# LayerNorm rows on ScalarE, shared low halves in eight blocks, a first x tile of its own, two counts ahead of a finish

## The reference, cut to what matters

```python
def reference(x, adj, W, b, gate_w, w1, w2, w3, sw1, sw2):   # x 2048x256, adj 2048x2048
    deg = maximum((adj != 0).sum(-1), 1)
    x = x + gnn(layernorm(x), adj, deg, W, b)
    x = x + ffn(layernorm(x), gate_w, w1, w2, w3, sw1, sw2)

def gnn(x, adj, deg, W, b):
    a_norm = rsqrt(deg) * (adj + eye) * rsqrt(deg)
    return relu((a_norm @ x + x) @ W + b)

def ffn(x, ...):                   # 8 experts of 256 -> 1024 -> 256, top 1, and a shared one
    comb = one_hot(argmax(x @ gate_w.T)) * softmax(its logit)
    y = sum over experts of (silu(x @ w1.T) * (x @ w3.T) * comb) @ w2.T
    return y + gelu(x @ sw1.T) @ sw2.T
```

## Time and profile before

| | us |
|---|---|
| median of 3 runs | 507.82 (506.71 to 508.75) |
| the profiled execution's own time | 510.69 |
| its span (first to last instruction) | 509.1 |
| PE busy, DVE, ACT, POOL | 457.6, 270.9, 197.2, 322.3 |
| mean granted clock of TensorE | 0.966 of full |

### The profile page before, as it was taken

How to read it: one execution, slowest core, us unless ns; L and a number is a source line. 1 busy time by engine, 2 the same in 40 slices (tenths; PEclk the granted TensorE clock), 3 DMA queues, 4 the chain that set the end, 5 groups by cost and what they waited for, 6 DMA issues and landing times.

```text
span 509.1 us, 8980 instructions
## 1 busy us (share of the span) xinstructions
PE 457.6 (90%) x2652; PEld 391.9 (77%) x2653; DVE 270.9 (53%) x558; ACT 197.2 (39%) x434; POOL 322.3 (63%) x299
## 2 busy tenths in 40 slices
PE   5899977999999989899687999699979999999992
PEld 5778756897789878798565888588868888888871
DVE  4997799917692569767451343233423333343330
ACT  3555721663456454745241333122322232232230
POOL 3889865487857786576065584857475848887111
PEclk9999989999999999999897999799989999999997
DMA  7574150503160251719869777787878787465000
GB/s 255 185 217 154 49 165 13 165 2 117 49 206 1 76 174 43 253 42 321 233 198 322 240 249 257 257 267 232 276 237 280 241 274 232 56 71 73 8 1 0
DMA packets 40876, 82.61 MB, mean 162 GB/s; under 512 B 4880, under 2 KB 16528, under 8 KB 38800
## 3 DMA queue, kind: packets, MB, share of 16 engines
q1 hardware_dynamic: 25792, 45.11, 28.8%
q0 software_dynamic: 7536, 29.39, 18.9%
q10 hardware_dynamic: 7520, 7.77, 4.9%
HBM read 74.74 MB, written 8.41 MB: 163 GB/s over the span
## 4 chain that ended last, share of the span: by engine, by line
PE 41%; DVE 15%; DMA 11%; POOL 10%; issue 6%; ACT 2%; SPq 1%; POOLq 0%; DVEq 0%; ACTq 0%
PE bank L1208 16%; DMA eraw<-in_experts 7%; POOL ering L413 6%; PE bank L1233 6%; PE bank L1126 5%; DVE count L729 4%; PE bank L1145 4%; DMA ering<-in_experts 4%; POOL a_lo L366 3%; DVE rows L705 3%; PE bank L1234 3%; PE bank L1219 2%; PE bank L1147 2%; PE bank L1040 1%; DVE resid L795 1%
## 5 line engine op out<-in xcount | busy, mean ns | idle before, releaser
L413 POOL TENSOR_TENSOR ering<-eraw,ering 128x512 fp32r<-128x512 f32 x84 | 105.7, 1286 | 75.1 <-DMA ering<-in_experts 37.4
L1208 PE MATMUL bank<-ering,xsT_hi 128*128 x368 | 125.8, 414 | 11.6 <-POOL ering L413 7.5
L366 POOL TENSOR_TENSOR a_lo<-araw,a_hi 128x512 fp32r<-128x512 f32 x64 | 93.6, 1480 | 30.3 <-ACT a_hi L500 30.1
L1040 PE MATMUL bank<-zz,a_hi 128*128 128x512 f32 (+1 forms) x256 | 93.3, 404 | 7.0 <-POOL a_lo L366 6.9
L1208 PEld LDWEIGHTS bank<-ering,xsT_hi 128*128 128x128 f32 x368 | 72.1, 196 | 29.4 <-issue 12.7
L959 DVE SCALAR_TENSOR_TENSOR hid<-bank,xs,sil 128x512 f32<-128x512 f32 x46 | 34.5, 751 | 111.0 <-ACT sil L625 109.0
L1208 PE MATMUL bank<-ering,xsT_lo 128*128 x184 | 75.0, 408 | 0.0
L625 ACT ACTIVATE sil<-bank 128x512 f32<-128x512 f32 x46 | 27.5, 599 | 119.7 <-PE bank L1208 119.7
L1042 PE MATMUL bank<-zz,a_lo 128*128 128x256 f32 (+1 forms) x256 | 72.2, 282 | 0.0
L1233 PE MATMUL bank<-ering,hidT_hi 128*128 x184 | 67.8, 408 | 1.2 <-DVE hidT_lo L967 1.2
L1040 PEld LDWEIGHTS bank<-zz,a_hi 128*128 128x128 f32 x256 | 48.8, 191 | 20.0 <-issue 8.4
(11 more groups left out here) (151 smaller groups left out, 809.4 us busy)
## 6 DMA issues: line engine op xcount, KB each, us to landing
eraw<-in_experts SPq DMA_DIRECT2D x96, 256.0 KB, 3.3
araw<-in_adj_t SPq DMA_DIRECT2D x32, 512.0 KB, 5.0
ering<-in_experts POOLq DMA_DIRECT2D x8, 1536.0 KB, 7.4
ering<-in_experts POOLq DMA_DIRECT2D x8, 1024.0 KB, 7.1
ering<-in_experts POOLq DMA_DIRECT2D x8, 512.0 KB, 5.9
xs<-sorted_x ACTq DMA_DIRECT2D x23, 129.0 KB
resid<-in_x SPq DMA_DIRECT2D x4, 512.0 KB, 8.8
sw_raw<-in_sw_t ACTq DMA_DIRECT2D x2, 1024.0 KB, 7.0
```

Of the source, the lines that this page charges most:

```text
L366: pool.tensor_tensor(a_lo[:, u % AR, :], araw[:, u // CJ, u % CJ, :], a_hi[:, u % AR, :].bitcast(F32), ALU.subtract).then_inc(adj_lo_ok, 1)
L413: pool.tensor_tensor(ering[:, slot, 1, c * ECW:(c + 1) * ECW], eraw[:, c % ER, :], ering[:, slot, 0, c * ECW:(c + 1) * ECW].bitcast(F32), ...
L1040: pe.matmul(acc(it)[:, :], a_hi[:, s, it * P:(it + 1) * P], zt, start=first, stop=False)
L1208: ins = pe.matmul(bank[2 * w + h][:, :], a[:, k, :], ering[:, bass.ds(slot, 1), part, at:at + BANK].rearrange("p a n -> p (a n)"), start=n ...
```

## The change

It has four parts.

- **Rows on ScalarE.** Except for the first four tiles, a norm's row is no longer a DVE instruction (L705) but an ACT one, `Identity(rstd * x + shift)` with two operands per partition. DVE makes `shift = -mean * rstd` for four tiles in one instruction (`scales`) after the reciprocal. In the front, ACT makes the row of tile t+2 after `z_high(t)`; for quarters 1 to 3 `stds` moves ahead of `a_hi` of tile 11, and the four rows come after that `a_hi`. For the last quarter the four rows come right after `stds`.
- **Low halves in eight blocks.** `sw1_lo` and the low half of `sw2_r` were one instruction each of 2048 elements. They become eight and eight of 256, each with its semaphore count; blocks 0 to 3 now after the second four counts of quarter 1, blocks 4 to 7 after `choose(0)`. PE waits for the blocks one by one; before, for all of them ahead of `gate(0)`.
- **First x tile alone.** SP loads x tile 0 (128 KB), chunk 0, x tiles 1 to 3 (384 KB), chunk 1, x group 1, chunk 2, group 2, chunk 3, group 3; before, group 0, group 1, chunk 0, group 2, chunk 1, group 3, chunk 2, chunk 3. ACT and DVE norm tile 0 alone, split W, split the transposed tile 0, and only then norm tiles 1 to 3. The rounding of the identity moves behind.
- **Two chunks counted ahead.** The first two of quarter 1's counts come before `finish_gnn(0)`.

```diff
-            rows_of_x(0)
+            sp.dma_start(resid[:, 0, :], x_in[0:P, :]).then_inc(x_first, 16)
             for c in range(NC):
-                if c + 1 < NQ:
-                    rows_of_x(c + 1)
                 chunk(0, c, c if c >= RAW else None)
+                if c == 0:
+                    sp.dma_start(resid[:, 1:QT, :], ...).then_inc(x_loaded[0], 16)
+                elif c < NQ:
+                    rows_of_x(c)
...
+            def scaled_rows(k, t):                                   # ScalarE
+                act.wait_ge(scale_ready, k)
+                act.activation(norm[:, t, :], resid[:, t, :], ACT.Identity, bias=shift[:, t % QT:t % QT + 1],
+                               scale=rstd[:, t % QT:t % QT + 1]).then_inc(ln_ready, 1)
...
-            stds(0)
-            act.wait_ge(consts, 1)
-            act.activation(ident_r[:], ident[:], ACT.Copy).then_inc(split_hi, 1)
+            stds(0, 0, 1)
             act.wait_ge(w_loaded, 16)
             act.activation(w_hi[:], w_raw[:], ACT.Copy).then_inc(split_hi, 1)
             xn_high(0)
+            stds(0, 1, QT)
...
                 z_high(t)
+                if QT <= t + 2 < NT:
+                    scaled_rows((t + 2) // QT, t + 2)
...
-                adj_highs(q, AR, TURN)
+                adj_highs(q, AR, TURN - 1)
                 stds(NQ + q - 1)
+                adj_highs(q, TURN - 1, TURN)
+                for t in range((q - 1) * QT, q * QT):
+                    scaled_rows(NQ + q - 1, t)
...
             stds(2 * NQ - 1)
+            for t in range((NQ - 1) * QT, NT):
+                scaled_rows(2 * NQ - 1, t)
...
+            def scales(k):                                           # VectorE
+                dve.wait_ge(std_ready, k + 2)
+                dve.wait_ge(ln_ready, k * QT)
+                chained(dve.reciprocal(rstd[:], std[:]))
+                settle()
+                dve.scalar_tensor_tensor(shift[:], mv[:, :, 0], -1.0, rstd[:], ALU.mult, ALU.mult
+                                         ).then_inc(scale_ready, 1)
...
-            dve.wait_ge(x_loaded[0], 16)
-            variances(group(0))
-            normalize(0, group(0))
+            dve.wait_ge(x_first, 16)
+            statistics(group(0), 0, 1)
+            aggregates(0, 1)
+            dve.wait_ge(std_ready, 1)
+            first_rows(0, 1)
...
             xn_low(0)
+            dve.wait_ge(x_loaded[0], 16)
+            statistics(group(0), 1, QT)
+            aggregates(1, QT)
+            dve.wait_ge(std_ready, 2)
+            first_rows(1, QT)
...
-                elif g < NQ:
-                    normalize(g, group(g), 2 * (i - 2), 2 * (i - 1))
+                elif g < NQ and i == 2:
+                    scales(g)
...
+            def split_blocks(first, last):
+                dve.wait_ge(split_hi, 5)
+                for ib in range(first, last):
+                    at = slice(ib * P, (ib + 1) * P)
+                    dve.tensor_tensor(sw1_lo[:, :, at], sw1_raw[:, :, at], sw1_hi[:, :, at].bitcast(F32),
+                                      ALU.subtract).then_inc(sw1_lo_ok, 1)
+                    dve.tensor_tensor(sw2_r[:, ib, 1, :], sw2_raw[:, ib, :], sw2_r[:, ib, 0, :].bitcast(F32),
+                                      ALU.subtract).then_inc(sw2_lo_ok, 1)
...
             inverse_degree(0)
+            count_chunks(1, 0, 2)
             finish_gnn(0)
             for q in range(1, NQ):
-                count_chunks(q, 0, RAW)
+                count_chunks(q, 2 if q == 1 else 0, RAW)
                 variances(group(q - 1))
                 if q == 1:
-                    split_shared()
-                normalize(NQ + q - 1, group(q - 1))
+                    split_gate()
+                scales(NQ + q - 1)
                 xfT_lows(q - 1)
                 count_chunks(q, RAW, NC)
+                if q == 1:
+                    split_blocks(0, NI // 2)
                 sum_halves(q)
...
                 choose(q - 1)
+                if q == 1:
+                    split_blocks(NI // 2, NI)
                 finish_gnn(q)
```

More of the change, by code:

```diff
@@ L109, in gnn_moe @@
     std = place("std", [P, QT], F32)
+    shift = place("shift", [P, QT], F32)
     deg = place("deg", [P, QT], F32)
@@ L204, in gnn_moe @@
         split_lo = sem("split_lo")
+        sw1_lo_ok = sem("sw1_lo_ok")
+        sw2_lo_ok = sem("sw2_lo_ok")
         dve_self = sem("dve_self")
@@ L509, in _ @@
             xn_high(0)
+            stds(0, 1, QT)
+            act.wait_ge(consts, 1)
+            act.activation(ident_r[:], ident[:], ACT.Copy).then_inc(split_hi, 1)
             LATER = (6, 9)
@@ L688, in statistics, with aggregates @@
                     chained(dve.bn_stats(stats[:, i, :], resid[:, tiles_of[i], :]))
-            def aggregates():
+            def aggregates(first=0, last=QT):
                 settle()
-                for i in range(QT):
+                for i in range(first, last):
                     dve.bn_aggr(mv[:, i, :], stats[:, i, :]).then_inc(var_ready, 1)
@@ L893, in _ @@
                     add_shared(2 * (q - 1) + 1)
-            dve.wait_ge(ln_ready, NT + (NQ - 1) * QT)
+            dve.wait_ge(scale_ready, 2 * NQ - 2)
             variances(group(NQ - 1))
-            normalize(2 * NQ - 1, group(NQ - 1))
+            scales(2 * NQ - 1)
             xfT_lows(NQ - 1)
```

45 lines of the change are left out of this document (25 added, 20 removed).

## The result

| | before | after |
|---|---|---|
| median of 5 runs | 507.82 us (506.71 to 509.07) | 512.28 us (510.08 to 514.13) |
| profiled execution | 510.69, span 509.1 | 510.08, span 508.5 |

The ratio is 1.0096, with a 95% interval from 1.0073 to 1.0119. The change makes the kernel slower by some 4.9 us. The forecast was 508.2, in a range up to 511.5.

What follows compares the result with a forecast made beforehand. PE was taken to set the end, holding 41% of the chain of waits, with DVE or POOL full in places. Terms 1.1 - 1.0 + 0.2 - 2.2 + 2.3 = +0.4 took 507.82 to 508.2 us, range 504.0 to 511.5.

Steps and rivals of the forecast that it cites:

- Quarter 1: Quarter 1 up to block 1: tile 8's gap goes, the finish slows beside POOL; middle taken, -1.0 us (-3 to +0.8).
- last norm: Last norm: ACT's wait for shift and four rows come before the table load, +2.3 us (1.6 to 2.6).
- first product: Start: transpose 1 stands ahead of product 0, which starts at 11.9 instead of 10.24, +1.65 us (1.0 to 2.0).
- rest of the front: Front after the first product: tile 4's row on ACT gives 0.3 us, the later two groups 0.25 together.
- blocks, and quarter 2's rows: The other four blocks after choose(0) may hold up POOL's gel_lo, +0.2 us; quarter 2's rows on ACT give -1.1.
- quarter 3: Quarter 3: rows on ACT are done sooner, so counts start and block 1 comes 1.1 us earlier.
- 0.25 given back: Front, tiles 8 and 12: two groups' waits shrink by 0.25 us together, net of shift and cycle (+1 to -1.6).
- The cover of blocks 0 to 3: Quarter 1: eight halves of about 0.34, 2.7 us in all, stand on DVE ahead of block 1; no clock term.
- the slower rival: Last norm and locks cost more; clock falls after waits from 3.27 us on; sum +3.7, 511.5 us; chance 0.23.
- Identity and the table: Rival: Identity needs its own table, loaded before and after each group's rows; 6 us or more, 514; chance 0.05.
- The shift always waits where POOL is busy: Front: by the skill's SBUF rule shift always waits for busy POOL, making the front +1.9 us instead of +1.1.
- the prediction's own signs of being wrong: Finish beside POOL stays at 6.3; ACT's rows are 0.3 apart and shift never waits; or last norm's clock falls.

Runs made afterwards that it cites:

- a_last_dve: The changed kernel with the last norm's four rows back on DVE; ratio 0.9999 to the kernel before.
- a_not_ahead: The changed kernel with all four first counts of quarter 1 behind finish_gnn(0) again; ratio 1.0066 to the kernel before.
- best5: The changed kernel with before's start, count order and last-norm rows; halves of blocks 0 and 1 after quarter 1's scales, 2 to 7 after choose(0); 0.9873 of before.
- best5_front_dve: best5 with the front's rows of groups 1 to 3 back on DVE; ratio 0.9902 to the kernel before.
- best1: Kernel before plus quarters 1 to 3's rows on ACT, two chunks counted ahead, all sixteen weight halves before quarter 1's transposes; ratio 0.9990 to before.

## Why the prediction was wrong

Forecast +0.4 at the end of the chain, measured +5.34 at the ranks and +4.9 by the ratio. Two steps failed. Quarter 1 was to give 1.0 and took 0.70, since the counts ahead pushed the finish beside POOL. And the granted clock behind PE's longer waits stood at nothing in the sum; it fell behind block 1, where stage 2 lost 1.5, and in the last norm, where the tail lost 0.9. The start, the front and the last norm had the right mechanism and too small a price, 0.8, 0.4 and 0.4. By the forecast's own terms:

| term | forecast | profile of after | what was missed |
|---|---|---|---|
| first product | +1.65 | +2.41 | bytes at 9.77, not 9.2; transposes at 0.66 |
| rest of the front | -0.55 | -0.15 | a cycle of 2.47; one `shift` held |
| quarter 1 | -1.0 | +0.70 | the finish took 9.5, not the middle |
| blocks, and quarter 2's rows | +0.2, -1.1 | +0.11 | the clock behind block 1's wait |
| quarter 3 | -1.1 | -1.35 | |
| last norm | +2.3 | +2.71 | 0.49 a row, and 0.2 for statistics that came later |
| clock behind it | in a rival | +0.90 | |

- **The start.** The mechanism was right (transpose 1 ahead of product 0, bytes late), the size off by 0.76: 0.57 for the landing, 0.17 from statistics to transpose, the rest in rounding.
- **The front.** "0.25 given back" was +0.43 from tile 4 to the end in this profile (37.32 to 37.75). The two parts of the price had been named, the cycle (2.42 forecast, 2.47 measured) and the shift that waits for POOL; it was there in one of three groups, as 0.70 instead of 0.16. Without it this part is -0.7 (36.66 in a_last_dve). The bounds that the prediction gives for the front, -0.6 to +2.6, don't follow from their parts, which add up to -0.3 and +3.3; the forecast doesn't rest on them.
- **Quarter 1** is the step that failed most. I let the gap of 3.27 go, credited DVE with 10.65 us less work, and took the middle between a finish that keeps its 6.3 and one that always waits. It took 9.5, and a_not_ahead shows what I hadn't asked: what the same kernel does without the counts ahead (3.5 less). The credit for work taken off DVE was real (a_not_ahead: q1 2.8 under before), and the counts ahead used it up.
- **The cover of blocks 0 to 3.** I put their 2.7 into DVE's sum ahead of block 1, and not what PE's wait there does to the clock, though the earlier trace rows had shown the pattern after a wait of 3.27 and I used it for the last norm. It cost 1.5 in stage 2 (53.46 against the 51.97 of a_last_dve).
- **Quarters 2 and 3.** Right in mechanism: -1.05 and -1.47 alone, for -1.1 each.
- **The last norm.** Right in place and order. The row's pitch was taken as 0.4 and is 0.49; four rows, 2.08, and the 0.44 for `shift` make 2.5. The Trainium skill's "ScalarE: Activation LUTs", section "What ACT_TABLE_LOAD costs", would have given it: 186 ns, twice 93 for the pointers and 0.833 for each of 256 elements are 585 ns, an estimate by that page, less an overlap of 93. The trace agrees: 598 ns for one row (mean of 28), 490 apart.
- **The clock after the last norm** stood only in the slower rival, at 0.9 and with a chance of 0.23. It fell in all six profiles that have the rows on ACT there, and cost 0.7 to 2.0 (tails of 13.8 to 15.1 against 13.1). That rival named the right mechanisms and came to 511.5; it had no term for stage 2. It let the clock fall only from a wait of 3.27 on; here it fell behind 2.0 to 2.4 and a second wait of 1.0 to 1.3. That the clock falls in the last norm was among the prediction's own signs of being wrong.
- **Identity and the table.** No table is loaded around the rows of the front or the quarters; that rival is out. The Trainium skill's "SBUF — State Buffer", section "Who interferes with whom", has instructions with two SBUF inputs contend with POOL's reads. The traces agree for the shift (0.16 alone; up to 1.11 behind an `a_lo`) and the halves (0.42 alone; 0.95 to 1.52). "The shift always waits where POOL is busy", as the prediction has it, is too much: it waited when it began inside an `a_lo`, and in after's front that was one of three.

## What to carry to other kernels

Price a wait of PE twice, once as its length and once as the granted clock behind it, wherever the change makes one longer: here waits of 2 to 3 us cost up to 2 us more than themselves, where PE set the pace behind them. A move that takes work off a full engine is worth nothing where the next thing in that engine's queue only moves into another engine's way. Try each part alone, since rows on ACT in mid kernel gave 2.2 us, and the same rows in the last norm took 3.5. DVE's idle time beside a running POOL was not free either, since the halves put there held POOL up (best1); put only as much there as the partner's own waits leave.

## What the runs showed of the hardware

- A DVE instruction of 4 elements a partition with two inputs in SBUF took 0.16 us, or up to 1.11 when POOL's 128x512 `a_lo` had begun 0.19 us or more before it: then it ended 0.02 us behind the `a_lo`'s end, in 38 of 38. In the front, through the queue behind it, one such hold of 0.70 cost PE some 1.1 us.
- DVE's halves of 256 took 0.42, or 0.95 to 1.52 when held by a `gel_lo` or `a_lo` of POOL that had begun 0.02 to 0.34 us before; the held ones ended 0.28 us behind its end. In best1 it was the other way round: an `a_lo` that began within a series of halves took 3.78, and the halves 0.42 each.
- After a PE wait of 1.6 us and eight transposes the clock stayed at 1.00 in six profiles of six; after one of 2.0 it fell in two of four; after 2.0 to 2.4 and a second one of 1.0 to 1.3 it fell in six of six. Before block 1 it fell behind 2.84 to 3.05 (five profiles), and not behind 2.38 and 2.50. The length alone doesn't decide: in the shared blocks behind quarter 1 it fell behind 1.17 (best5) and not behind 1.04 (best5_front_dve).
